# GpSimd instead of SyncE issues the condition blocks of the first four tiles

## The reference

```
y[b]  = W_cond[itok[b]]^T x[b]                  # (64 x 64) times (64 x 1024), per sample
out   = x + y @ W_up^T                          # 4096 rows of y, 1024 x 1024 weights
          + LoRA of the expert that scores best # 4 experts of rank 8, logits = y @ gate_w^T + bias
```

## Time and profile before

| | us |
|---|---|
| median of 3 runs | 406.57 (406.15 to 406.83) |
| the profiled execution, its own time | 406.41 |
| its span, first to last instruction | 404.6 |
| TensorE busy | 398.1 (98% of the span) |
| VectorE / ScalarE / GpSimd busy | 301.7 / 110.2 / 132.4 |
| granted TensorE clock | 0.999 of full speed |

### The profile page before, as it was taken

The page is one execution under the profiler, slowest core; times in us unless marked ns, Lnnn a source line. Parts: engine busy times, 40 slices in busy tenths (PEclk is TensorE's granted clock), DMA queues, the critical chain, the costliest instruction groups (busy, mean ns, idle before and its releaser), DMA issues.

```text
span 404.6 us, 9746 instructions
## 1 busy us (share of the span) xinstructions
PE 398.1 (98%) x3451; PEld 357.3 (88%) x3451; DVE 301.7 (75%) x717; ACT 110.2 (27%) x226; POOL 132.4 (33%) x123
## 2 busy tenths in 40 slices
PE   7999999999999999999999999999999999999997
PEld 7898988979888898888979798898988889798996
DVE  3899668889876858776696766867677766967675
ACT  5896211323114031211213131131311303131310
POOL 1689211628031250505205080221605043050700
PEclk9999999999999999999999999999999999999999
DMA  7910240503214132313125031150322221250102
GB/s 251 358 58 2 83 139 28 190 26 113 79 67 151 39 100 105 132 56 103 54 83 186 28 109 70 40 183 26 110 104 89 99 78 58 104 181 28 54 33 98
DMA packets 20993, 39.39 MB, mean 97 GB/s; under 512 B 7494, under 2 KB 7750, under 8 KB 20970
## 3 DMA queue, kind: packets, MB, share of 16 engines
q1 hardware_dynamic: 17600, 27.40, 18.6%
q10 hardware_dynamic: 3370, 11.69, 9.1%
HBM read 22.30 MB, written 16.78 MB: 97 GB/s over the span
## 4 chain that ended last, share of the span: by engine, by line
PE 96%; DMA 1%; SPq 1%; ACT 1%; issue 0%; DVE 0%
PE bank_y L878 23%; PE bank_x L878 22%; PE bank_b L878 11%; PE bank_c L929 10%; PE y_ps L791 7%; PE bank_c L1083 5%; PE bank_b L1083 4%; PE bank_x L856 2%; DMA cond_pair<-in_L_cond_weights_dram 1%; PE bank_c L878 1%; PE bank_b L884 1%; PE bank_x L884 1%; PE bank_y L884 1%; PE bank_c L884 1%; PE bank_y L856 1%; PE y_ps L1157 1%
## 5 line engine op out<-in xcount | busy, mean ns | idle before, releaser
L878 PE MATMUL bank_y<-w_s,hl_s 128*128 128x292 f32 (+1 forms) x384 | 51.5, 290 | 0.0
L878 PEld LDWEIGHTS bank_y<-w_s,hl_s 128*128 128x128 f32 x384 | 49.2, 188 | 2.5 <-issue 2.5
L878 PE MATMUL bank_x<-w_a,hl_a 128*128 128x256 f32 (+1 forms) x384 | 50.8, 288 | 0.0
L878 PEld LDWEIGHTS bank_x<-w_a,hl_a 128*128 128x128 f32 x384 | 49.5, 188 | 0.3 <-issue 0.2
L878 PE MATMUL bank_b<-w_s,hl_s 128*128 128x512 f32 x192 | 47.7, 397 | 0.1
L878 PE MATMUL bank_y<-w_a,hl_a 128*128 128x292 f32 x360 | 47.7, 288 | 0.0
L878 PEld LDWEIGHTS bank_y<-w_a,hl_a 128*128 128x128 f32 x360 | 46.6, 188 | 0.3
L307 POOL TENSOR_TENSOR s_sum<-a 128x512 f32<-128x512 f32 x9 | 11.9, 1328 | 102.4 <-DVE a L1403 101.9
L878 PE MATMUL bank_x<-w_s,hl_s 128*128 128x292 f32 x336 | 44.6, 289 | 0.0
L929 PE MATMUL bank_c<-w_s,hl_s 128*128 128x512 f32 x168 | 44.4, 409 | 0.0
L307 POOL TENSOR_TENSOR s_sum<-a,a_even 128x512 f32<-128x512 f32 x7 | 9.1, 1297 | 106.1 <-DVE a_even L1403 106.1
(11 more groups left out here) (194 smaller groups left out, 622.0 us busy)
## 6 DMA issues: line engine op xcount, KB each, us to landing
out_dram<-x_sb SPq DMA_DIRECT2D x63, 256.0 KB, 2.0
x_sb<-in_x_dram ACTq DMA_DIRECT2D x22, 512.0 KB, 3.6
x_sb<-in_x_dram SPq DMA_DIRECT2D x10, 512.0 KB, 3.3
w_raw<-in_L_ffn_W_up_dram SPq DMA_DIRECT2D x8, 512.0 KB, 5.7
cond_pair<-in_L_cond_weights_dram SPq DMA_DIRECT2D x64, 16.0 KB, 2.8
out_dram<-x_sb SPq DMA_DIRECT2D x2, 128.0 KB, 1.9
router_sb<-in_L_ffn_lora_A_dram ACTq DMA_DIRECT2D x1, 128.0 KB
lora_b_sb<-in_L_ffn_lora_B_dram SPq DMA_DIRECT2D x1, 128.0 KB, 5.2
```

Of the source, the lines that this page charges most:

```text
L878: mm = pe.matmul(dst, hl[op][:, a, k, :], w[:, b, k, cols], start=(fresh and k == 0 and a + b == 0), stop=(k == KH - 1 and a == 1), skip_g ...
```

## The change

The eight blocks of the first four tiles are no longer issued by SyncE but by GpSimd. GpSimd now waits for the index list and for the zeroing of `cond_pair`, reads each index and issues the DMA: the blocks of tile 0 before the constants of `rank_w`, those of tiles 1, 2 and 3 right behind them, all ahead of GpSimd's first low part. They count on semaphores of their own (`first_pair_loaded`), and the later loads, which stay with SyncE, count from zero.

```diff
+        first_pair_loaded = [sem(f"first_pair_loaded{s}") for s in range(4)]
...
-            def load_first_pair(q, t):
-                sp.wait_ge(index_loaded, 16)
-                sp.wait_ge(pair_zero, 1)
-                load_pair(q, q, t)
-
...
             sp.dma_start(x_sb[:, 0, :], x_pairs[0]).then_inc(x_loaded[0], 16)
-            load_first_pair(0, 0)
             load_w_up(5)
             load_w_up(2)
             load_w_up(6)
-            load_first_pair(0, 1)
             sp.dma_start(x_sb[:, 1, :], x_pairs[1]).then_inc(x_loaded[1], 16)
...
-            load_first_pair(1, 0)
             sp.dma_start(x_sb[:, 2, :], x_pairs[2]).then_inc(x_loaded[2], 16)
-            load_first_pair(1, 1)
             sp.dma_start(x_sb[:, 3, :], x_pairs[3]).then_inc(x_loaded[3], 16)
...
             pool.memset(cond_pair[:, :, :], 0.0).then_inc(pair_zero, 1)
+
+            def load_first_pair(q, t):
+                pool.wait_ge(index_loaded, 16)
+                pool.wait_ge(pair_zero, 1)
+                for b in range(2):
+                    at = 4 * q + 2 * t + b
+                    rows = slice(b * C, (b + 1) * C)
+                    index = pool.value_load(index_sb[0:1, at:at + 1], min_val=0, max_val=S - 1)
+                    pool.dma_start(cond_pair[rows, 2 * q + t, b * D:(b + 1) * D],
+                                   cond_weights[bass.ds(index, 1), :, :].rearrange("s c d -> (s c) d"))\
+                        .then_inc(first_pair_loaded[2 * q + t], 16)
+
+            load_first_pair(0, 0)
             for e in range(E):
                 pool.memset(rank_w[:, e:e + 1], float(E - e)).then_inc(const_done, 1)
+            load_first_pair(0, 1)
+            load_first_pair(1, 0)
+            load_first_pair(1, 1)
...
-                pe.wait_ge(pair_loaded[2 * par + t], 16 * (q - par) + 32)
+                pe.wait_ge(pair_loaded[2 * par + t], 16 * (q - par))
...
-                pe.wait_ge(pair_loaded[t], 32)
+                pe.wait_ge(first_pair_loaded[t], 32)
```

## The result

The changed kernel takes 407.95 us (median; 406.78 to 408.48, 20 runs), the kernel before 406.76 us beside it (406.13 to 408.08, 20 runs). The ratio is 1.0023 (1.0015 to 1.0031): slower by 0.94 us. The profiled execution took 407.97 us. Two runs of the kernel before in a later set, of 554 and 646 us at a granted clock of 0.66 and 0.56, are left out of all ratios.

A forecast was written before the change was run, and what follows sets the result against it. TensorE, busy 398.1 of 404.6 us, bounds the kernel; only the first 43 us change. Queue 0, GpSimd's work 0 and moved transfers against the wait's gain sum to +0.1 us: 406.7 us median, range 406.0 to 410.4.

The forecast's parts named there:

- the bound that the prediction set for slower: Whole kernel: slower by over 0.2%, given a chance of 0.45.
- a late GpSimd: Rival, chance 0.27: eight issues delay GpSimd's low parts and LoRA steps; 409.7 us at 1.9 us a block.
- GpSimd's first low part by 14.1 us: Sign in the changed profile: GpSimd's eight issues end in time for its first low part to start by 14.1 us.
- the wait was named by `cond_pair` and not by `x_sb`: Sign at L801: TensorE's wait would be named by `x_sb` and end between 10.3 and 10.7 us.
- SyncE's queue gets shorter: SyncE's early issues: each block pair costs it 2.9 us, but off the path, so taken as 0.
- The wait for the blocks goes: Tile 0's first `y`: pair 0 lands well before 10 us; gain 0.34 us at most, 0.2 left at 15.6 us.
- the change doesn't do what it says: Case: GpSimd's blocks of tile 0 land after 10.5 us, the wait stays; time about that of before.
- The transfers move: DMA stream: pairs move ahead of tiles 0 and 1 of `x`, 0.12 us each; sum +0.1 us at tile 1.
- GpSimd's work starts later: GpSimd before its first low part: 1.46 us a block, through at 13.7 us, inside the cover, so 0.
- the far bound: GpSimd's issue price: 2.25 us a block if an issue occupies it like one of its 128x512 operations, 1.27 us.
- the estimate with the 1 us in it: GpSimd's issues with 1 us in place of 0.48: 1.98 us a block, free at 17.8 us, about 410.3 us.
- Small packets slow the stream: Rival, chance 0.18: GpSimd's packets slow the DMA stream, a pair costs 0.9 us; 409.8 us, or 408.2 at half.

The follow-up runs named there:

- e1: The changed kernel with ten matmuls on zeros ahead of tile 0's `y`, filling TensorE's idle time; 407.07 us, ratio 1.0007 to the kernel before.
- e2: The kernel before with the same matmuls of zeros ahead of tile 0's `y`; 406.81 us, ratio 1.0002.
- e3: The changed kernel with tile 0's two blocks given back to SyncE behind tile 0 of `x`; 408.29 us, ratio 1.0036.
- e4: The kernel before with only tile 0's two blocks issued by GpSimd, tiles 1 to 3 on SyncE; 407.98 us, ratio 1.0021.
- e5: The kernel before with SyncE issuing tile 0's blocks ahead of tile 0 of `x`; 407.04 us, ratio 1.0011.
- e6: The kernel before with the bias transfer moved behind the LoRA rounding, near 20 us; 406.78 us, ratio 1.0014.
- e7: The changed kernel with SyncE waiting for an earlier transfer to land before each of four loads; 407.90 us, ratio 1.0027.
- e8: The kernel before with tile 0's blocks issued by ScalarE behind its bias load, the others by SyncE; 407.95 us, ratio 1.0037.
- e9: The changed kernel with the bias transfer issued near 20 us; 405.93 us, ratio 0.9970 to the kernel before.
- e10: The kernel before with the bias near 20 us and tile 1 of `x` issued ahead of tile 1's blocks on SyncE; 406.24 us, ratio 0.9979.

## Why the prediction was right, and where it was not

The time, 407.95 us, is in the range given (406.0 to 410.4), and the change is worth little, as forecast. But it lies 0.65 us above the forecast's own range (406.2 to 407.3), and at a ratio of 1.0023 (1.0015 to 1.0031) it is just past the bound that the prediction set for slower, with the bound inside the interval. That the whole range holds it is luck: its upper part was there for a late GpSimd and for a stream slowed by GpSimd's packets, and neither is what happened. Of the signs that the prediction named, GpSimd's first low part by 14.1 us came true; the wait was named by `cond_pair` and not by `x_sb`, `y` of tile 1 started at 17.29 and not at 15.6 to 15.8 us, and the `lora_b` transposes at 23.60 and not at about 22.1. Step by step:

- *SyncE's queue gets shorter, worth 0: right.* Row 5 of `W_up` is issued at 2.75 us instead of 5.54, and lands at 11.8 us instead of 11.4. Nothing that TensorE waits for came earlier by it. It has a worth once the stream ahead has room, as the version with the late bias shows.
- *The wait for the blocks goes: wrong.* "Pair 0 should land well before 10 us" is the step that failed. The blocks landed at 11.17 us, and in the five other kernels that issue some of the blocks from a second queue and keep the bias at its place, the last block of tile 0 came at 10.99 (twice), 11.15, 11.36 and 11.69 us. What I took for the price of standing behind 2 MB in SyncE's queue was not that: with nothing ahead of it in GpSimd's queue the block begins to move no earlier, just behind 9 us, and takes longer. The prediction did list this case ("the change doesn't do what it says"), but held that the wait could then be no longer than before unless the stream was slower too. That was wrong as well: the block is later by 0.45 us in the filled version and 0.63 in the profiled one, tile 0 of `x` by only 0.15 and 0.41.
- *The transfers move, 0.12 us a pair: the sizes are near at tile 0, but not for the reason given.* Tile 0 of `x` was to land at 10.44 us, with two pairs ahead of it; it landed at 10.61 in the profiled execution and at 10.35 in the filled version, and it was issued 0.13 us later in both (2.27 against 2.14 us). No two pairs were ahead of it: none of GpSimd's packets moved before 9 us, and tile 1's blocks landed at 11.95 and 12.47 us. Nor is a pair 128 packets there, as the prediction took it: on GpSimd's queue it is 64. Tile 1 was to land at 15.6 us and did at 15.95, and at 16.22 in the filled version. It did not decide in the profiled execution, where TensorE had been held up for longer, but in the filled version TensorE waited 0.48 us for it: this term was put too low.
- *GpSimd's work starts later, hidden: right.* 1.35 us a block against 1.46 taken, 12.94 us against 14.1 allowed. The rival in which it is late (0.27) did not happen. Its issue does occupy GpSimd, 0.52 us each, but the operation at the far bound (1.27 us) was far too dear, and so was the 1.98 us a block of the estimate with the 1 us in it.
- *Small packets slow the stream (0.18): the mechanism is real, in the wrong place.* While ScalarE's packets for the bias move, the engines' share is 0.72; with the bias moved away it is 1.05. GpSimd's packets do nothing like it: 392 GB/s at a share of 1.00 in the changed kernel from 10.7 to 17 us, 416 in the filled version as before, and the 98% above. The Trainium skill's page "DMA: Bandwidth & Descriptors", section Queues, rings and completion order, says that an engine takes turns between its queues packet by packet. The spread of GpSimd's 44 packets beside SyncE's 160 from 9 to 10.5 us agrees with that, but the loss beside the bias is not explained by it: the bias's packets take 2.5% of the engines' time and SyncE's 69.9%, and the missing 28% is idle time, which turns alone don't give. From 6.5 to 9 us the profiled changed kernel moves 170 GB/s and the filled version 194, before 222; GpSimd's queue moves nothing in that time, so it is not its packets taking turns, and why it is less is open. Section Issuing engines are not separate DMA queues says that another issuing engine saves only the sequencer's time, and the trace agrees in that nothing else was saved; it was worth something only in the version where the bias was gone from the first 10 us.
- *The clock: missing.* No step of the prediction asked what TensorE's clock does if a wait gets longer. That is the larger part of the loss, about 0.6 of 0.94 us, and the fill took it away. The other part, 0.3 to 0.4 us between the medians at full clock, fits the later block and the later tile 1 of `x`: in the filled version `y` of tile 0 starts 0.45 us later than before and `y` of tile 1 1.0 us later. No experiment parts these two.

Of each profiled execution, in us: when the later block of tile 0 and tile 1 of `x` had landed (issue plus time to landing), when their `y` starts, the granted clock of the whole execution, and its own time.

| kernel | block | `y` of tile 0 | tile 1 of `x` | `y` of tile 1 | clock | time |
|---|---|---|---|---|---|---|
| before | 10.54 | 10.68 | 15.38 | 15.63 | 0.999 | 406.41 |
| changed | 11.17 | 11.30 | 15.95 | 17.29 | 0.996 | 407.97 |
| e1, changed, filled | 10.99 | 11.13 | 16.22 | 16.64 | 1.000 | 407.25 |
| e2, before, filled | 10.39 | 10.53 | 15.37 | 15.78 | 1.000 | 406.57 |
| e3, tile 0's blocks back | 11.15 | 11.29 | 16.17 | 16.41 | 1.000 | 407.15 |
| e4, only tile 0's | 10.99 | 11.13 | 17.44 | 17.68 | 1.000 | 408.31 |
| e5, blocks before `x` | 8.32 | 10.71 | 15.82 | 16.87 | 0.995 | 407.53 |
| e6, late bias | 9.25 | 9.39 | 15.98 | 16.22 | 0.996 | 408.60 |
| e7, paced | 11.36 | 11.50 | 16.75 | 17.66 | 0.996 | 408.25 |
| e8, ScalarE | 11.69 | 11.82 | 16.77 | 17.01 | 1.000 | 407.95 |
| e9, both | 9.95 | 10.09 | 15.24 | 15.48 | 1.000 | 406.43 |
| e10, without GpSimd | 9.37 | 9.51 | 14.95 | 15.42 | 1.000 | 406.27 |

The time follows the start of `y` of tile 1, not that of tile 0. Only e6 stands apart, and there the clock falls at that very place and not before it.

What stays open: why the blocks that GpSimd issues at 3.74 and 4.92 us move nothing before 9 us (seven packets in e4), and why giving tile 0's blocks back to SyncE did not restore 5.5 us. With the bias late, GpSimd's packets move before 9 us (52 of them) and its second block of tile 0 takes 5.0 us, so the bias has a part in what holds it, but the cause is not isolated. In every kernel that issues the blocks behind `x` and has the bias at its place, the later block landed between 0.3 and 1.2 us after `x`, and no experiment here tells what fixes that distance. Also open is why row 1 of `W_up` lands at 7.8 us in one execution and at 9.0 in another, and why the clock falls in only some runs of the same kernel.

## What to carry to other kernels

Before a load is given to another engine so that it is issued earlier, read from the trace whether it is late because it was issued late, or because the DMA engines are full of something ahead of it: here it was issued as early and came later. Then see when the next transfers are used: the time of these kernels follows the start of `y` of tile 1, which the prediction put down as 0.1 us. Look in that stretch for a queue with many packets and no bytes, and ask when its data is wanted; taking it out moved tile 0 of `x` by 1.3 us, though it shortened the kernel (by 0.2 or 0.3%) only together with an earlier issue of tile 1. And where a wait of TensorE grows or a second one comes close to it, price in the granted clock too: the runs in which it fell were 1.1 us slower than the others, three times what the lateness itself costs.

## What the hardware showed that I had not expected

- The granted clock fell to half after idle times of 1.49 and 1.10 us with 1.1 us of transposes between them; 11 of 20 runs of this kernel had the lower mean clock and were 1.1 us slower. With ten small matmuls in the gap, none of 12 did. In two other profiled executions it fell after a single wait, of 1.55 us (e5, 0.51 from 12.5 to 15.2 us) and of 1.70 us (e6, 0.56 from 16 to 19.5 us), but in three with waits of 1.48, 1.35 and 1.52 us (e3, e4, e8) it stayed at 1.00, although 5 of 6, 5 of 12 and 2 of 5 runs of these kernels had a reduced clock. The waits of those runs are not on record.
- In the profiled executions before and after, the two blocks of tile 0 (16 KB each) begin to move just behind 9 us whether SyncE or GpSimd issued them. On SyncE's queue they are through by 10 us, on GpSimd's, beside SyncE's full one, 44 of their 64 packets are by 10.5 us.
- The load of the bias, 2 KB, takes 7.8 us to land, and while it moves the engines' share is 0.72 for 2.5 us: without it 411 GB/s instead of 222.
- In the kernels in which GpSimd issues DMAs, SyncE's first loads go out 0.13 us later (tile 0 of `x` at 2.27 instead of 2.14 us); where ScalarE issued the blocks instead, it was 2.15.
